# A Mamba-and-FFN block on one core: x*D joins the transposed y on the matrix engine, and the gate product moves from GpSimd to VectorE

## The chip, the cores and the metric

The kernel runs on one core of a Trainium2 chip. The core has five engines that run side by side and meet only through semaphores: PE (TensorE, matrix products into PSUM), DVE (VectorE), ACT (ScalarE), POOL (GpSimd, which cannot reach PSUM here) and SP, whose queue issues most of the transfers. The metric is the device time of one execution in microseconds (us); lower is better.

## The reference, cut to what matters

Four sequences of 1024 tokens with 512 features pass an FFN with ternary weights, a Mamba layer, and the same FFN again. The part around the change is the end of the Mamba layer, for 1024 inner channels (E) and 16 states (N):

```python
def step(h, inp):
    d_l, B_l, C_l, x_l = inp
    A_bar = jnp.exp(d_l[:, :, None] * A)
    h = h * A_bar + (d_l * x_l)[:, :, None] * B_l[:, None, :]
    y_l = jnp.einsum('ben,bn->be', h, C_l)
    return (h, y_l)
...
y_apply_D = y + x * W_D
y_skip = y_apply_D * _silu(skip)
return resid + y_skip @ W_out
```

## The kernel before, in words

The 4096 tokens are cut into 16 chunks of 256 (`CH`). A software pipeline treats three chunks in one round: `PREV` jobs finish chunk i-1, `THIS` jobs belong to chunk i, `NEXT` jobs prepare chunk i+1. The rounds are called fill, first, loop (14 times, i = 1 to 14), last and drain. Each round has 32 slots. The tables `LOOP_SLOTS`, `FIRST_SLOTS` and so on set, slot by slot, which jobs PE runs, and the other engines derive their own fixed order from the same tables. Nothing is reordered at run time.

A job on PE fills one of four PSUM banks (`NBANK`). `bank_ready[bk]` tells that PE has filled it, `bank_used[bk]` that its reader is done. Names of jobs: `U1_p`/`G1_p` and `U2_p`/`G2_p` are the FFN's up and gate products (line 1596), `DN1`/`DN2` the down products (line 1607), `IN_q` and `SK_q` the projections to x and to the skip gate (line 1619), `DB` the projection to delta, B and C (line 1629), `OM_t` the output projection (line 1668).

The scan runs in 32 steps per chunk (`STEPS`): 16 states for the first half of the channels, then 16 for the second. For each step POOL writes u*B into the ring `h` (line 778; line 784 adds the carried state), DVE scans it in two pieces (line 1342), and then there are two ways to C*h. In most steps PE transposes h (line 1553) and DVE adds it with its C to `y` (line 1364). In the steps listed in `ELEM` (nine per chunk, the last of the first half being step 15, the last of the second half step 31) POOL multiplies h by a plane of C (line 795) and a transfer that it issues adds the product to `xw` (line 799); `elem_added` tells of its landing. `xw` begins as x*D, written by ACT (line 980).

`y` has tokens on partitions, everything else channels. So each half of `y` is transposed back at its end by PE, in four quarters of 256 channels, jobs `YT_0` to `YT_3` (line 1659): four 128x128 transposes each. In the loop `YT_0` stands in slot 20, `YT_1` in slot 21, `YT_2` in slot 4 and `YT_3` in slot 5 of the next round. DVE adds the bank to `xw` (`y_plus_x`, line 1433), POOL multiplies `xw` by the gate into `gz` (`gated`, line 906), and `out_proj` waits for that with `z_ready`.

POOL also forms the low half `hl` of the hidden activations (line 884), once DVE has multiplied the gate product in (line 1380) and ACT has written the high half `hh` (line 1064). Its orders tie POOL to PE: POOL's `hl` of `G1_7` comes in slot 11, after PE's `G1_7` in slot 10, and the product and transfer of step 15 in POOL's slot 19. Likewise `hl` of `G1_1` comes in POOL's slot 2, and step 31 in slot 3.

Of the kernel before, what the change touches and what calls it, by code (L numbers as in the profile page):

```python
# [21 lines left out]
P = 128  # L22
D, E, F, N, DD = 512, 1024, 2048, 16, 128
# [3 lines left out]
CH = 256  # L27
TB = CH // P
NCH = TOK // CH
# [15 lines left out]
QT = EB // 2  # L45
# [265 lines left out]
def after(ph, name, lag, s):  # L311

    return name in PHASES[ph] and s == USE_OF[ph][name] + lag
# [37 lines left out]
def elems_before(c, s):  # L351

    whole = [len(elem_of(k)) for k in range(c)]
    return sum(whole) + sum(k < s for k in elem_of(c))
# [38 lines left out]
def job_no(ph, i, name):  # L393

    p = BANK_OF[ph][name]
    size = {f: len(JOBS[f, p]) for f in PHASES}
    before = JOBS[ph, p].index(name)
    if ph != "fill":
        before += size["fill"]
    if ph == "loop":  # L400
        before = before + size["first"] - size["loop"] + size["loop"] * i
    elif ph in ("last", "drain"):
        before += size["first"] + size["loop"] * (NCH - 2) + (size["last"] if ph == "drain" else 0)
    return p, before


def phase_of(c):

    return "first" if c == 0 else ("last" if c == NCH - 1 else "loop")
# [27 lines left out]
    return 2 * NCH - 1 + (0 if ph == "last" else 1)  # L437


def need(eng, sem, value):  # L440

    if isinstance(value, int) and value <= 0:
        return
    eng.wait_ge(sem, value)


def macaron_kernel(nc, resid, norm_w, W_skip, W_in, conv_w, conv_b, W_delta_1, W_delta_2, b_delta_2, W_B, W_C,
# [3 lines left out]
    ALU = mybir.AluOpType  # L451
# [8 lines left out]
    with ctx:  # L460
# [3 lines left out]
        def sem(name):  # L464
            return ctx.enter_context(nc.semaphore(name))
# [18 lines left out]
        ident = sb("ident", [P, P])  # L484
# [45 lines left out]
        xw = sb("xw", [P, EB, CH])  # L530
        gz = sb("gz", [P, EB, CH])
# [8 lines left out]
        y = sb("y", [P, TB, HE * P])  # L540
# [19 lines left out]
        bank_ready = [sem(f"bank_ready{p}") for p in range(NBANK)]  # L560
# [16 lines left out]
        conv_begun, conv_step, edge_added = sem("conv_begun"), sem("conv_step"), sem("edge_added")  # L577
        ctanh_ready, xc_ready, xw_ready = sem("ctanh_ready"), sem("xc_ready"), sem("xw_ready")
        sp_step, delta_ready, u_ready = sem("sp_step"), sem("delta_ready"), sem("u_ready")
        gtanh_ready, z_ready = sem("gtanh_ready"), sem("z_ready")  # L580
        pool_go, dve_go, act_go = sem("pool_go"), sem("dve_go"), sem("act_go")
        pe_go, sp_go = sem("pe_go"), sem("sp_go")

# [151 lines left out]
        def _(pool):  # L735
# [4 lines left out]
            pl = nc.gpsimd  # L740
# [151 lines left out]
                pl.tensor_tensor(u[:, :, :], delta[:, half * HE:(half + 1) * HE, :],  # L892
                                 xc[:, half * HE:(half + 1) * HE, :], ALU.mult).then_inc(u_ready, 1)

            def gated(ph, i, q):

                bk, before = job_no(ph, i, f"YT_{q}")
                need(pool, bank_used[bk], before + 1)
                gate = f"SK_{q}"
                if q < 2:  # L900
                    bk, before = job_no(ph, i, gate)
                else:
                    bk, before = job_no(phase_of(i - 1), i - 1, gate)
                need(pool, bank_used[bk], before + 1)
                qb = slice(2 * q, 2 * q + 2)
                pl.tensor_tensor(gz[:, qb, :], xw[:, qb, :], gz[:, qb, :], ALU.mult).then_inc(z_ready, 1)  # L906

            def run(ph, i):
                has = PHASES[ph]
                scan = "SK_0" in has  # L910
                next_ln = NEXT_LN_FILL if ph == "fill" else NEXT_LN
                for s in range(STEPS):
                    coming, done = step_of(ph, i, s + U_AHEAD), step_of(ph, i, s)
                    if coming and s not in UB_LATE:
                        u_times_b(*coming)
                    if done and is_elem(*done) and s not in ELEM_LATE:
                        state_times_c(*done)
                    if s == EDGES_AT and "IN_0" in has:
                        edges(i + 1)
                    for half in range(2):  # L920
                        if after(ph, f"IN_{2 * half + 1}", 0, s):
                            add_edges(ph, i, half)
                    if after(ph, "OM_1", 0, s):
                        rstd(ph, i, "2")
                    for q in range(QT):
                        if after(ph, f"YT_{q}", 0, s):
                            gated(ph, i, q)
                    for kind, p in hidden_units(ph, s):
                        hidden_low(ph, i, kind, p)
                    if after(ph, "DN1_1", 0, s):  # L930
                        rms(ph, i)
                    if ph != "fill" and after(ph, "D2_1", 2, s):
                        softplus(i + 1, 0)
                    if ph != "fill" and after(ph, "D2_1", 3, s):
                        first_state(i + 1, 0)
                    if after(ph, "D2_3", 2, s):
                        softplus(i, 1)
                    if after(ph, "D2_3", 3, s):
                        first_state(i, 1)
                    if s == next_ln and "T1_0" in has:  # L940
                        rstd(ph, i, "n")
                    if coming and s in UB_LATE:
                        u_times_b(*coming)
                    if done and is_elem(*done) and s in ELEM_LATE:
                        state_times_c(*done)
# [8 lines left out]
        def _(sc):  # L954
# [19 lines left out]

            def x_times_d(i, half):

                need(sc, z_ready, 4 * i - 2 + 2 * half)
                need(sc, xc_ready, 2 * i + 2)
                for b in range(half * HE, (half + 1) * HE):
                    ins = ac.activation(xw[:, b, :], xc[:, b, :], ACT.Copy, scale=wd[:, b:b + 1])  # L980
                ins.then_inc(xw_ready, 1)
# [266 lines left out]
        def _(ve):  # L1248
# [173 lines left out]
                gg = gz[:, 2 * q:2 * q + 2, :].rearrange("p e t -> p (e t)")  # L1422
                v.scalar_tensor_tensor(out=gg, in0=gg, scalar=1.0, in1=pp, op0=ALU.add, op1=ALU.mult).then_inc(bank_used[bk], 1)

            def y_plus_x(ph, i, q):

                bk, pp = ready(ph, i, f"YT_{q}")
                qb = slice(2 * q, 2 * q + 2)
                c = i if q < 2 else i - 1
                need(ve, xw_ready, 2 * c + q // 2 + 1)  # L1430
                need(ve, elem_added, 16 * elems_before(c, N * (q // 2 + 1)))
                yx = xw[:, qb, :]
                ins = v.tensor_tensor(yx.rearrange("p e t -> p (e t)"), pp, yx.rearrange("p e t -> p (e t)"), ALU.add)  # L1433
                ins.then_inc(bank_used[bk], 1)

            def run(ph, i):
                if ph == "first":
# [28 lines left out]
            def use(ph, i, name):  # L1466

                nslot = (i + 1) % XSLOTS
                pslot = (i - 1) % XSLOTS
                t = int(name[-1]) if "_" in name else 0  # L1470
                if name[0] == "U":
                    hidden_up(ph, i, int(name[1]), t)
                elif name[0] == "G":
                    hidden_gate(ph, i, int(name[1]), t)
                elif name[:2] in ("T1", "T2"):
                    x_low(ph, i, int(name[1]), t)
                elif name[:2] == "OM":
                    need(ve, x12_ready, i)
                    add_to_stream(ph, i, name, pslot, 0.5)
                    stats(ph, i, "2", pslot, t)  # L1480
                    if t:
                        moments(ph, i, "2")
                elif name[:3] == "DN1":
                    add_to_stream(ph, i, name, nslot, down_sc[:, 0:1])
                    stats(ph, i, "p", nslot, t)
                    if t:
                        moments(ph, i, "p")
                elif name[:3] == "DN2":
                    add_to_stream(ph, i, name, pslot, down_sc[:, 0:1])
                elif name[:2] == "SK":  # L1490
                    skip_gate(ph, i, t)
                elif name[:2] == "YT":
                    y_plus_x(ph, i, t)

            def background(ph, i, s):

# [19 lines left out]
        def _(pe):  # L1516
# [135 lines left out]
            def y_T(ph, i, q):  # L1652
                c = i if q < 2 else i - 1
                for t in range(TB):
                    need(pe, y_added[t], rows_before(c, N * (q // 2 + 1)))
                bk, pp = opened(ph, i, f"YT_{q}")
                for e in range(2):
                    for t in range(TB):
                        ins = te.transpose(pp[:, e * CH + t * P:e * CH + (t + 1) * P],
                                           y[:, t, (2 * (q % 2) + e) * P:(2 * (q % 2) + e + 1) * P], ident[:, :])  # L1660
                ins.then_inc(bank_ready[bk], 1)

            def out_proj(ph, i, name, lo, hi):
                t = int(name[3])
                bk, pp = opened(ph, i, name, lo)
                need(pe, z_ready, 4 * i - 3 + (hi - 1) // 2)
                for e in range(lo, hi):
                    ins = te.matmul(pp, gz[:, e, t * P:(t + 1) * P], w_out[:, e, :], start=(e == 0), stop=(e == EB - 1))  # L1668
                if hi == EB:
                    ins.then_inc(bank_ready[bk], 1)  # L1670
# [94 lines left out]
```

## Time and profile before

| what | value |
|---|---|
| median of 3 runs | 2801.0 us (2798.93 to 2805.9) |
| profiled execution, first to last instruction | 2796.2 us |
| PE busy | 2614.3 us (93%) |
| DVE busy | 2447.7 us (88%) |
| POOL busy | 2382.1 us (85%) |
| ACT busy | 1879.0 us (67%) |
| mean granted PE clock | 0.979 of 2.4 GHz |

The profiled execution is known by its span; the timed runs have no trace. Busy time is the union of an engine's instructions. A matmul on f32 operands appears as two records, one on 16-bit or 8-bit operands, or a transpose, as one. The duration of a PE record contains its latency, so that records overlap; what a matmul occupies is read from how far apart the starts of equal ones lie. In the chain of work that ended last, pieces of one kind are merged and do not overlap.

### The profile page before, as it was taken

To read this page: it belongs to the slowest core of one execution; us is meant where nothing else is said; L and a number is where in the kernel's file an instruction comes from. 1 tells how busy PE (TensorE), PEld (TensorE's weight loads), DVE (VectorE), ACT (ScalarE), POOL (GpSimd) and SP (SyncE) were. 2 spreads that over 40 slices of the span, in tenths; PEclk is the share of its full clock that TensorE was granted. 3 is DMA by queue.
4 is the path that set the end of the run, shared out by engine and by line. 5 is a ranking of instruction groups with operands and counts; after the bars stand their busy time and mean duration, and the time that the engine had idled before them with its cause. 6 is when DMAs were issued, how large, how long until landed. Compare 5 with 4: busy or idle time off the path is not lost.

```text
span 2796.2 us, 51718 instructions
## 1 busy us (share of the span) xinstructions
PE 2614.3 (93%) x17439; PEld 2021.6 (72%) x17439; DVE 2447.7 (88%) x3221; ACT 1879.0 (67%) x4340; POOL 2382.1 (85%) x2023
## 2 busy tenths in 40 slices
PE   5776899999999999999999999999999999999878
PEld 4555677777878777786777778677777877776655
DVE  4378899999999999899999999899999999999892
ACT  7374867676676767667676766767676676767651
POOL 1168899999898999999998999999999898999881
PEclk9898999999999999999999999999999999999989
DMA  7013222223222322222232222222222222222220
GB/s 274 31 55 72 60 61 76 56 58 83 59 74 60 80 50 65 77 63 73 58 81 53 70 69 63 73 63 75 54 72 66 66 69 65 73 57 68 64 55 8
DMA packets 94446, 192.44 MB, mean 69 GB/s; under 512 B 12588, under 2 KB 32232, under 8 KB 93672
## 3 DMA queue, kind: packets, MB, share of 16 engines
q0 software_dynamic: 20304, 73.93, 13.7%
q1 hardware_dynamic: 73880, 115.21, 13.0%
q8 instruction: 141, 2.31, 0.3%
q14 instruction: 121, 0.99, 0.1%
HBM read 106.26 MB, written 8.91 MB: 41 GB/s over the span
## 4 chain that ended last, share of the span: by engine, by line
POOL 41%; PE 32%; issue 12%; DVE 7%; ACT 2%; DMA 1%; POOLq 1%; DVEq 0%; ACTq 0%
POOL h L778 22%; PE ps L1596 10%; POOL h L795 7%; PE ps L1607 6%; PE ps L1619 6%; POOL hl L884 4%; PE ps L1553 4%; PE ps L1668 4%; DVE h L1342 3%; POOL u L892 2%; POOL delta L849 2%; DVE xc L1400 1%; PE ps L1629 1%; POOL h L784 1%; POOL xw L799 1%
## 5 line engine op out<-in xcount | busy, mean ns | idle before, releaser
L778 POOL TENSOR_TENSOR h<-u,bb 128x1024 f32<-128x1024 f32 x512 | 1257.8, 2466 | 27.2 <-DVE u L1417 14.2
L1342 DVE TENSOR_TENSOR_SCAN h<-ps,h 128x512 f32<-128x512 f32 x1024 | 1191.8, 1207 | 36.5 <-POOL h L784 18.6
L1037 ACT ACTIVATE ps<-delta,a_neg 128x255 f32<-128x255 f32 x2048 | 873.1, 468 | 377.0 <-DVE h L1342 374.8
L1596 PE MATMUL ps<-xh,q_up 128*128 128x256 f16 x2048 | 466.5, 275 | 36.1 <-DVE xl L1280 19.1
L1364 DVE SCALAR_TENSOR_TENSOR y<-ps,ccur,y 128x512 f32<-128x512 f32 x678 | 471.4, 738 | 6.9 <-PE ps L1553 6.3
L1596 PE MATMUL ps<-xh,q_gate 128*128 128x256 f16 x2048 | 462.7, 273 | 8.1 <-DVE xw L1433 7.8
L1596 PE MATMUL ps<-xl,q_up 128*128 128x256 f16 x2048 | 466.5, 275 | 0.0
L1596 PE MATMUL ps<-xl,q_gate 128*128 128x256 f16 x2048 | 462.4, 273 | 0.0
L1553 PE MATMUL ps<-ident,h 128*128 128x128 f32 x2968 | 398.2, 277 | 50.2 <-DVE y L1364 46.7
L1553 PEld LDWEIGHTS ps<-ident,h 128*128 128x128 f32 x2968 | 344.6, 142 | 112.7 <-issue 50.9
L884 POOL TENSOR_TENSOR hl<-act,hh 128x512 f16<-128x512 f32 x256 | 314.5, 1229 | 97.3 <-ACT hh L1064 94.4
L1607 PE MATMUL ps<-q_down,hh 128*128 128x512 fp8e4 x1024 | 388.6, 379 | 2.5 <-POOL hl L884 1.2
L1607 PE MATMUL ps<-q_down,hl 128*128 128x512 fp8e4 x1024 | 388.5, 379 | 0.0
L795 POOL TENSOR_TENSOR h<-h,cplane 128x1024 f32<-128x1024 f32 x141 | 334.8, 2374 | 0.0
L1059 ACT ACTIVATE act<-ps,tanh_sc 128x512 f32<-128x512 f32 x256 | 174.9, 683 | 201.1 <-PE ps L1596 129.0
L1372 DVE SCALAR_TENSOR_TENSOR act<-act,ps 128x512 f32<-128x512 f32 x256 | 173.6, 678 | 98.3 <-ACT act L1059 97.9
L1596 PEld LDWEIGHTS ps<-xh,q_up 128*128 128x128 fp8e4 x2048 | 201.6, 98 | 76.8 <-issue 51.8
L1619 PE MATMUL ps<-xrT,w_in 128*128 128x256 f32 x1024 | 235.3, 384 | 13.5 <-DVE xc L1400 11.2
L1668 PE MATMUL ps<-w_out,gz 128*128 128x512 f32 x512 | 243.5, 609 | 2.3 <-POOL gz L906 2.2
L1596 PEld LDWEIGHTS ps<-xh,q_gate 128*128 128x128 fp8e4 x2048 | 200.9, 98 | 39.8 <-issue 15.0
L1619 PE MATMUL ps<-xrT,w_skip 128*128 128x256 f32 x1024 | 229.5, 379 | 0.0
L1596 PEld LDWEIGHTS ps<-xl,q_up 128*128 128x128 fp8e4 x2048 | 201.6, 98 | 33.5 <-issue 4.6
(126 smaller groups left out, 3642.9 us busy)
## 6 DMA issues: line engine op xcount, KB each, us to landing
xw<-h POOLq DMA_DIRECT2D x141, 512.0 KB, 4.5
bb<-b_scratch SPq DMA_DIRECT2D x224, 256.0 KB, 3.1
cplane<-c_scratch SPq DMA_DIRECT2D x141, 128.0 KB, 3.1
xs<-in_L_attn_resid_dram SPq DMA_DIRECT2D x17, 512.0 KB, 3.5
out_dram<-xs SPq DMA_DIRECT2D x15, 512.0 KB, 4.3
wraw<-in_L_ffn_W_up_dram SPq DMA_DIRECT2D x4, 1024.0 KB, 9.6
wraw<-in_L_ffn_W_gate_dram SPq DMA_DIRECT2D x4, 1024.0 KB, 12.3
wraw<-in_L_ffn_W_down_dram SPq DMA_DIRECT2D x4, 1024.0 KB, 14.1
```

What stands on the lines that cost most here:

```text
L778: ins = pl.tensor_tensor(hs, u[:, :, :], bb[:, q % 2, s % PLANES:s % PLANES + 1, :].broadcast_to([P, HE, CH]), ALU.mult)
L795: pl.tensor_tensor(hs, hs, cplane[:, k:k + 1, :].broadcast_to([P, HE, CH]), ALU.mult).then_inc(times_c, 1)
L884: pl.tensor_tensor(hl[:, 2 * p:2 * p + 2, :], act[:, p % ACTS, :].rearrange("q (f t) -> q f t", f=2), hh[:, 2 * p:2 * p + 2, :], ALU.subtr ...
L1037: ins = ac.activation(abar[r][:, e, 1:], delta[:, k, 1:], ACT.Exp, scale=a_neg[:, k, n:n + 1])
L1059: ac.activation(act[:, p % ACTS, :], pp, ACT.Tanh, scale=tanh_sc[:, 0:1]).then_inc(tanh_ready, 1)
L1342: v.tensor_tensor_scan(hr, abar[r].rearrange("p e t -> p (e t)"), hr, 0.0, ALU.mult, ALU.add).then_inc(scanned, 1)
L1364: ins = v.scalar_tensor_tensor(out=yy, in0=hT[:, t, :], scalar=cc, in1=yy, op0=ALU.mult, op1=ALU.add)
L1553: ins = te.transpose(hT[:, t, e * P:(e + 1) * P], h[:, (STEPS * i + s) % RING, e, t * P:(t + 1) * P], ident[:, :])
L1596: ins = te.matmul(pp[:, f * CH:(f + 1) * CH], w[:, d, col:col + P], part[:, d, :], start=(d == 0 and part is xh), stop=(d == DB - 1 and pa ...
L1607: ins = te.matmul(pp, part[:, f, t * P:(t + 1) * P], q_down[:, f, :], start=(f == 0 and part is hh), stop=(f == FB - 1 and part is hl))
L1619: ins = te.matmul(pp[:, e * CH:(e + 1) * CH], w[:, d, col:col + P], xrT[:, d, :], start=(d == 0), stop=(d == DB - 1))
L1668: ins = te.matmul(pp, gz[:, e, t * P:(t + 1) * P], w_out[:, e, :], start=(e == 0), stop=(e == EB - 1))
```

## The change

The x*D with the elementwise states (`xw`) is no longer added by DVE. PE makes each quarter's transposition as four ordinary f32 products with the identity, the first of which opens the bank's accumulation, waits for `xw_ready` and `elem_added`, and adds `xw` by a fifth product, identity times `xw`, 128x512 in f32. DVE then multiplies the bank by the gate straight into `gz`, and POOL's product is gone with its semaphore. `out_proj` now waits for DVE's `bank_used`, and ACT's `x_times_d` for PE's `bank_ready` of the quarters of the chunk before.

```diff
-            def gated(ph, i, q):
...
-                pl.tensor_tensor(gz[:, qb, :], xw[:, qb, :], gz[:, qb, :], ALU.mult).then_inc(z_ready, 1)
...
             def x_times_d(i, half):
-                need(sc, z_ready, 4 * i - 2 + 2 * half)
+                if i:
+                    for q in (2 * half, 2 * half + 1):
+                        bk, done = y_T_of(i - 1, q)
+                        need(sc, bank_ready[bk], done + 1)
...
-            def y_plus_x(ph, i, q):
+            def gated(ph, i, q):
                 bk, pp = ready(ph, i, f"YT_{q}")
...
-                need(ve, xw_ready, 2 * c + q // 2 + 1)
-                need(ve, elem_added, 16 * elems_before(c, N * (q // 2 + 1)))
-                yx = xw[:, qb, :]
-                ins = v.tensor_tensor(yx.rearrange("p e t -> p (e t)"), pp, yx.rearrange("p e t -> p (e t)"), ALU.add)
-                ins.then_inc(bank_used[bk], 1)
+                gate, done = job_no(ph, i, f"SK_{q}") if q < 2 else job_no(phase_of(i - 1), i - 1, f"SK_{q}")
+                need(ve, bank_used[gate], done + 1)
+                gg = gz[:, 2 * q:2 * q + 2, :].rearrange("p e t -> p (e t)")
+                v.tensor_tensor(gg, pp, gg, ALU.mult).then_inc(bank_used[bk], 1)
...
             def y_T(ph, i, q):
...
-                        ins = te.transpose(pp[:, e * CH + t * P:e * CH + (t + 1) * P],
-                                           y[:, t, (2 * (q % 2) + e) * P:(2 * (q % 2) + e + 1) * P], ident[:, :])
+                        te.matmul(pp[:, e * CH + t * P:e * CH + (t + 1) * P],
+                                  y[:, t, (2 * (q % 2) + e) * P:(2 * (q % 2) + e + 1) * P], ident[:, :], start=(e, t) == (0, 0), stop=False)
+                need(pe, xw_ready, 2 * c + q // 2 + 1)
+                need(pe, elem_added, 16 * elems_before(c, N * (q // 2 + 1)))
+                ins = te.matmul(pp, ident[:, :], xw[:, 2 * q:2 * q + 2, :].rearrange("p e t -> p (e t)"), start=False, stop=True)
                 ins.then_inc(bank_ready[bk], 1)
...
             def out_proj(ph, i, name, lo, hi):
...
-                need(pe, z_ready, 4 * i - 3 + (hi - 1) // 2)
+                gate, done = y_T_of(i - 1, (hi - 1) // 2)
+                need(pe, bank_used[gate], done + 1)
```

The slot tables are the same, so every job keeps its place. On PE, in a loop round, around `YT_2` and `YT_3` (ahead of them stands the gate product `G1_3`, between them the transposes of one scan step, behind them `U1_4`), there stood before:

```order
L1596 MATMUL ps<-xl,q_gate 128x256
L1659 MATMUL ps<-ident,y 128x128 x4
L1553 MATMUL ps<-ident,h 128x128 x8
L1659 MATMUL ps<-ident,y 128x128 x4
L1596 MATMUL ps<-xh,q_up 128x256
```

and there stand now (line 1650 is the four products on y, line 1654 the one on xw):

```order
L1587 MATMUL ps<-xl,q_gate 128x256
L1650 MATMUL ps<-ident,y 128x128 x4
L1654 MATMUL ps<-xw,ident 128x512
L1544 MATMUL ps<-ident,h 128x128 x8
L1650 MATMUL ps<-ident,y 128x128 x4
L1654 MATMUL ps<-xw,ident 128x512
L1587 MATMUL ps<-xh,q_up 128x256
```

Two 128x512 products have come in, each behind a wait for the transfers into xw, and everything behind them on PE waits with them.

On POOL, in a loop round, at the place of `YT_0` and `YT_1` (from the last transfer of the first half on), there stood before:

```order
L799 DMA xw<-h 128x1024
L884 TENSOR_TENSOR hl<-act,hh 128x512
L778 TENSOR_TENSOR h<-u,bb 128x1024
L784 TENSOR_TENSOR h<-h,a 128x4
L877 TENSOR_TENSOR xc<-xc,edge 128x4x3
L906 TENSOR_TENSOR gz<-xw,gz 128x512
L778 TENSOR_TENSOR h<-u,bb 128x1024
L784 TENSOR_TENSOR h<-h,a 128x4
L795 TENSOR_TENSOR h<-h,cplane 128x1024
L799 DMA xw<-h 128x1024
L906 TENSOR_TENSOR gz<-xw,gz 128x512
```

The two rows of line 906 are gone and the rest stands in the same order.

## Rows read from the trace of the kernel before

**Rows 1.** The page's head and its busy times.

```profile
span 2796.2 us, 51718 instructions
PE 2614.3 (93%) x17439; PEld 2021.6 (72%) x17439; DVE 2447.7 (88%) x3221; ACT 1879.0 (67%) x4340; POOL 2382.1 (85%) x2023
```

**Rows 2.** The page's chain that ended last, by engine.

```profile
POOL 41%; PE 32%; issue 12%; DVE 7%; ACT 2%; DMA 1%; POOLq 1%; DVEq 0%; ACTq 0%
```

**Rows 3.** Busy time, ten rounds: length, PE, PEld, DVE, ACT, POOL, granted clock, DMA share.

```profile
400.00:2025.60 1625.60, 1598.51 (x10763) 1240.43 (x10762) 1503.75 (x1981) 1142.15 (x2684) 1499.20 (x1274) 1.00 0.27 67
```

**Rows 4.** Timeline of PE (start, length): YT_0 of rounds 1 and 11.

```profile
399.88 0.60 PE L1659 MATMUL ps<-ident,y 128*128 128x128 f32 x4
...
2025.49 0.60 PE L1659 MATMUL ps<-ident,y 128*128 128x128 f32 x4
```

**Rows 5.** Groups by line: busy us, mean ns, idle before it.

```profile
L906 POOL TENSOR_TENSOR gz<-xw,gz 128x512 f32<-128x512 f32 x64 | 81.9, 1314 | 25.5 <-DVE xw L1433 25.5
L1433 DVE TENSOR_TENSOR xw<-ps,xw 128x512 f32<-128x512 f32 x64 | 43.5, 682 | 5.5 <-DMA xw<-h 4.7 <-PE ps L1659 0.8
L1659 PE MATMUL ps<-ident,y 128*128 128x128 f32 x256 | 40.0, 281 | 8.9 <-DVE y L1364 4.7 <-ACT tmp L1116 3.7
```

**Rows 6.** Chain in order of time: start, us, records.

```profile
1007.28 0.86 PE ps L1668 x2
1008.14 0.88 PE ps L1553 x8
...
1022.43 6.91 PE ps L1619 x32
...
1079.70 4.35 PE ps L1629 x32
```

**Rows 7.** Timeline of POOL, round 5: hl of G1_7, and step 15's transfer.

```profile
1008.50 1.16 POOL L884 TENSOR_TENSOR hl<-act,hh 128x512 f16<-128x512 f32 x1
...
1049.22 0.89 POOL L799 DMA_DIRECT2D xw<-h  x1 [0.57 <-POOL h L795]
```

**Rows 8.** Timelines of DVE and ACT between G1_7 and that hl.

```profile
1003.50 0.69 DVE L1380 SCALAR_TENSOR_TENSOR act<-ps,act 128x512 f32<-128x512 f32 x1
1004.11 2.33 DVE L1342 TENSOR_TENSOR_SCAN h<-ps,h 128x512 f32<-128x512 f32 x2
...
1007.38 0.61 ACT L1064 ACTIVATE hh<-act 128x512 f16<-128x512 f32 x1
```

**Rows 9.** Timeline of PE, round 5: first product behind G1_7, and YT_0.

```profile
1003.22 0.38 PE L1607 MATMUL ps<-q_down,hh 128*128 128x512 fp8e4 x1
...
1050.01 0.60 PE L1659 MATMUL ps<-ident,y 128*128 128x128 f32 x4
```

**Rows 10.** The page's transfers: issues, KB each, median us to landing.

```profile
xw<-h POOLq DMA_DIRECT2D x141, 512.0 KB, 4.5
```

**Rows 11.** Timelines of POOL and PE: step 31's transfer, and YT_2.

```profile
969.38 0.89 POOL L799 DMA_DIRECT2D xw<-h  x1 [0.57 <-ACT carry L1043]
...
971.76 0.63 PE L1659 MATMUL ps<-ident,y 128*128 128x128 f32 x4
```

**Rows 12.** The same two for step 15 and YT_0 of round 4.

```profile
885.62 0.88 POOL L799 DMA_DIRECT2D xw<-h  x1 [0.57 <-POOL h L795]
...
888.19 0.60 PE L1659 MATMUL ps<-ident,y 128*128 128x128 f32 x4
```

**Rows 13.** Two idle times of PE, and busy times with granted clock around each.

```profile
737.73 2.64 PE L1619 MATMUL ps<-xrT,w_in 128*128 128x256 f32 x11 [1.98 <-DVE xc L1400]
2581.50 1.22 PE L1553 MATMUL ps<-ident,h 128*128 128x128 f32 x8 [4.14 <-DVE y L1364]
...
733.00:753.00 20.00, 17.76 (x136) 14.38 (x134) 19.82 (x30) 12.95 (x31) 17.54 (x14) 1.00 0.31 66
2577.00:2600.00 23.00, 13.03 (x54) 7.64 (x52) 17.34 (x19) 14.09 (x40) 21.05 (x16) 0.85 0.40 103
```

**Rows 14.** Who ended PE's idle time before line 1668.

```profile
  POOL gz L906: 9.6, 16
```

More of the change, by code:

```diff
@@ L437, in rstd_run, with y_T_of @@
     return 2 * NCH - 1 + (0 if ph == "last" else 1)
+def y_T_of(c, q):
+    i = c if q < 2 else c + 1
+    ph = {0: "first", NCH - 1: "last", NCH: "drain"}.get(i, "loop")
+    return job_no(ph, i, f"YT_{q}")
 def need(eng, sem, value):
@@ L579, in macaron_kernel @@
         sp_step, delta_ready, u_ready = sem("sp_step"), sem("delta_ready"), sem("u_ready")
-        gtanh_ready, z_ready = sem("gtanh_ready"), sem("z_ready")
+        gtanh_ready = sem("gtanh_ready")
         pool_go, dve_go, act_go = sem("pool_go"), sem("dve_go"), sem("act_go")
@@ L893, in u_of @@
                                  xc[:, half * HE:(half + 1) * HE, :], ALU.mult).then_inc(u_ready, 1)
-            def gated(ph, i, q):
[L897 to L905, printed above, removed]
-                pl.tensor_tensor(gz[:, qb, :], xw[:, qb, :], gz[:, qb, :], ALU.mult).then_inc(z_ready, 1)
             def run(ph, i):
@@ L924, in run @@
                         rstd(ph, i, "2")
-                    for q in range(QT):
-                        if after(ph, f"YT_{q}", 0, s):
-                            gated(ph, i, q)
                     for kind, p in hidden_units(ph, s):
@@ L1423, in skip_gate @@
                 v.scalar_tensor_tensor(out=gg, in0=gg, scalar=1.0, in1=pp, op0=ALU.add, op1=ALU.mult).then_inc(bank_used[bk], 1)
-            def y_plus_x(ph, i, q):
+            def gated(ph, i, q):
                 bk, pp = ready(ph, i, f"YT_{q}")
-                qb = slice(2 * q, 2 * q + 2)
-                c = i if q < 2 else i - 1
-                need(ve, xw_ready, 2 * c + q // 2 + 1)
-                need(ve, elem_added, 16 * elems_before(c, N * (q // 2 + 1)))
-                yx = xw[:, qb, :]
-                ins = v.tensor_tensor(yx.rearrange("p e t -> p (e t)"), pp, yx.rearrange("p e t -> p (e t)"), ALU.add)
-                ins.then_inc(bank_used[bk], 1)
+                gate, done = job_no(ph, i, f"SK_{q}") if q < 2 else job_no(phase_of(i - 1), i - 1, f"SK_{q}")
+                need(ve, bank_used[gate], done + 1)
+                gg = gz[:, 2 * q:2 * q + 2, :].rearrange("p e t -> p (e t)")
+                v.tensor_tensor(gg, pp, gg, ALU.mult).then_inc(bank_used[bk], 1)
             def run(ph, i):
@@ L1492, in use @@
                 elif name[:2] == "YT":
-                    y_plus_x(ph, i, t)
+                    gated(ph, i, t)
             def background(ph, i, s):
```

## The prediction

> **What bounds the kernel now.** I began with the page's busy times [rows 1]: PE, DVE and POOL all stand between 85% and 93%, so the average decides nothing. The chain that ended last runs 41% through POOL and only 32% through PE [rows 2], which would make POOL the engine to relieve. But such a chain follows one of several paths of nearly equal length, so I looked at the steady rounds alone. Two equal events ten rounds apart give the round: (2025.49 - 399.88)/10 = 162.56 us [rows 4]. In the same ten rounds PE is busy for 1598.5 of 1625.6 us at full clock: 2.7 us of idle time in a round [rows 3]. DVE has 12.2 us and POOL 12.6 us. PE's records overlap, so its busy time might flatter it; but starts lie as close as the column count allows (next part), so PE is really streaming. PE is the fullest engine and has 2.7 us to give; POOL is tied to it through the ring and through `hl`, which is how the chain comes to run there.
>
> **The change part by part.**
>
> *POOL loses 64 products.* They are 81.9 us busy and had 25.5 us of waiting before them [rows 5], in a steady round 4 x 1.3 = 5.1 us. That is 5.1 us more of slack on an engine that already has 12.6.
>
> *DVE swaps one operation for another.* The add of a bank and an SBUF tile, 128x512 f32, takes 682 ns [rows 5]; the product has the same operands and sizes. Price 0. Its wait for the transfers (4.7 us in all) goes, and comes back on PE.
>
> *PE gets the work.* Prices come from pieces of the chain [rows 6]. An f32 product of 512 columns is two records in 0.86 us; 256 columns: 16 products in 6.91 us, 0.432 each; 160 columns: 16 products in 4.35 us, 0.272 each. That is 1.69 ns a column at all three sizes. Transposes of 128 columns go at 0.88/8 = 0.11 us. An f32 product of 128 columns does not occur in the steady rounds. Below it cannot beat the column law, 0.218 us; above, the product of 160 columns, with the same size of weights, bounds it at 0.272. I take 0.218, since all three sizes lie on the law. A quarter then costs 4 x 0.218 + 0.86 - 4 x 0.11 = 1.29 us more (1.51 at the upper bound). A round has four: 5.2 us (6.0). I add 0.2 us a round for the extra switches between operand types, an allowance of mine, bounded by the same 0.8.
>
> A page's rule speaks here. The Trainium skill, page "TensorE: Matmul & The Clock Gate", section "Terms", says that transpose mode is four times faster for FP32, while the rows say twice (0.218 against 0.11). By the page's factor a product would take 0.44 us and a quarter 2.18 us; no f32 product of 128 columns is in this trace, but the one of 160 columns at 0.272 contradicts it.
>
> *PE waits for the transfers.* The fifth product now stands in PE's queue behind `elem_added`, and the next gate product, then everything else, stands behind it. YT_0 in round 5: step 15's transfer is issued at 1049.22 [rows 7], lands a median 4.5 us later [rows 10], at 1053.7. PE starts YT_0 at 1050.01 [rows 9] and with the slower products is ready for the fifth at 1050.88. So PE would wait 2.8 us. Can POOL, with its new slack, be earlier? POOL's 40.7 us from `hl` of G1_7 to that issue [rows 7] are a closed run of its own work and contain none of the removed products. That `hl` starts at 1008.50, and its input ends at 1007.99 [rows 8]: it can move by 0.5 us. The input itself hangs on PE: DVE's product starts with the end of G1_7 (behind it PE's next job starts at 1003.22 [rows 9]), then come DVE's scan of the next step (2.33 us), ACT's exponentials and `hh`, in fixed order [rows 8]. So this wait is not a matter of load but of a path from PE back to PE: 1003.2 to 1053.7 is 50.5 us, less 0.5, against 47.7 us of PE's own work. The wait is 2.3 us. In the three rounds that begin a sequence (4, 8, 12) POOL has no line 784 and issues earlier: 885.62 + 4.5 = 890.1 against 888.19 + 0.87 = 889.1 [rows 12], 1.0 us. Mean over 14 rounds: (11 x 2.3 + 3 x 1.0)/14 = 2.0 us; I take 2.2, since some landings will be later than the median. YT_1 needs no later transfer and does not wait.
>
> YT_2: issued at 969.38, landed at 973.9; PE starts at 971.76 and is ready at 972.63 [rows 11]. 1.3 us, and again a short path from G1_1 through DVE, ACT and POOL's `hl`, in which POOL may gain about half a microsecond. I take 0.7 us (0 to 1.3).
>
> *What is given back.* PE no longer waits for POOL's product ahead of `out_proj`: 9.6 us in 16 rounds, 0.6 a round [rows 14]. Some of the other 2.1 us of PE's idle time will shrink as DVE and POOL have more slack; but idle time inside the two paths above gives nothing, since the wait grows by as much. I take 0.8 in all (0 to 2).
>
> *ACT's wait* moves from `z_ready` to `bank_ready` of jobs that ended at least three slots before. Price 0.
>
> *Sum.* A loop round: 5.2 + 0.2 + 2.2 + 0.7 - 0.8 = 7.5 us, 14 rounds 105 us. Eight of the 64 quarters lie in first, last and drain, 8 x 1.29 = 10.3 us, where PE is not full; I take 8. Together +113 us against the span of 2796.2, giving 2909. The median of the runs shown lies 4.8 us above that span, so the time is 2801 + 113 = 2914 us.
>
> **The rivals.**
>
> *POOL leads and the waits vanish.* If the lighter POOL ran 2 to 3 us further ahead, only the work would stay: 5.2 - 0.8 + 0.2 = 4.6 a round, 64 us, plus 8: 2873 us; with the waits half gone, 2893. For it: POOL would be relieved by 5.1 us just where the chain runs. Against: the closed run of POOL work above, and its start tied to G1_7.
>
> *The clock falls.* PE idle for 1.98 us kept full clock; after idling 4.14 us the stretch around it shows 0.85 of it [rows 13], between the levels 2.4 and 1.2 GHz: 0.15 x 23 = 3.4 us lost. The new wait of 2.3 us lies nearer to the first row. If every YT_0 did as the second, 14 x 3.4 = 48 us more: 2962. A late landing in a round or two could do it there alone, for 3 to 7 us.
>
> *The dearer product.* With 0.272 us it is 14 us more: 2928. By a factor of four, taken as a mechanism of this kernel, 4 x (0.44 - 0.218) x 64 = 57 us more: 2971. The product of 160 columns speaks against it. This is the page's rule above.
>
> *Not slower.* POOL is the pacer, as the chain suggests, PE's added work hides in its idle time, and the round becomes shorter by POOL's 5.1 us: 14 x 5.1 = 71 us, 2730. It would need PE to take 5.2 us more inside a round of 157.5 us, where it now fills 159.9. With PE's extra work just covered, the time stays 2801. It decides if PE has more than 5.2 us free per round; the rows give 2.7.
>
> **How the numbers follow.** The forecast with its waits (2890 to 2945): 0.60. Waits mostly gone (2865 to 2890): 0.20. Clock or dearer product (2945 to 2975): 0.14. Not slower, 0.04; something I have missed above that, 0.02. The range 2868 to 2955 goes from the vanishing waits, nearly bare, to the forecast with the dearer product and both waits unhelped: 14 x (6.0 + 2.6 + 1.3) + 10 = 149, with 4.8 us of clock loss. About 0.3% (8 us) is what a measurement of this kernel can tell from no change. Faster by more than that 0.02, within it 0.03, slower 0.95.
>
> **What would show each step right or wrong.** After the change the ten rounds should give about 170 us a round. PE's idle time before the fifth product should be near 2.2 us at YT_0 and 0.7 us at YT_2, released by the transfer into `xw`, shorter in rounds 4, 8 and 12. The fifth product should occupy 0.86 us, the four before it 0.22 each. POOL's idle time should rise by about 12 us a round, and the chain should pass through the transfer once a round. No idle time before the fifth product would speak for the first rival; a granted clock under 1.00 in rounds 2 to 14 for the second; a distance of 0.27 or 0.44 us between the products on y for the third; a round of 163 us or less would make the whole reading wrong.

## The result, and the profile after

The changed kernel takes 2943.0 us (median of 4 runs, 2942.5 to 2944.5) against 2800.8 before: a ratio of 1.051, 95% interval 1.049 to 1.052, so 142 us slower. The forecast was 113 us slower, 2914 us, with a range of 2868 to 2955 that holds the result.

The page of the changed kernel, its head, its busy times and the chain that ended last by engine:

```profile
span 2941.5 us, 52422 instructions
PE 2721.4 (93%) x17823; PEld 2090.7 (71%) x17823; DVE 2457.5 (84%) x3221; ACT 1882.0 (64%) x4340; POOL 2314.9 (79%) x1959
...
POOL 47%; PE 22%; issue 14%; DVE 6%; DMA 3%; ACT 2%; POOLq 1%; DVEq 0%; ACTq 0%
```

Beside [rows 1]: PE is busy for 107 us more, POOL for 67 us less, DVE for 10 and ACT for 3 us more. Beside [rows 2] the chain leans on POOL even more, though POOL has less to do, and the share of transfers in it has gone from 1% to 3%. A chain through POOL did not mean that work taken from POOL would shorten it.

The timeline of PE at YT_0 of rounds 1 and 11, and the busy times between them (columns as in [rows 3]):

```profile
410.63 0.61 PE L1650 MATMUL ps<-ident,y 128*128 128x128 f32 x4
...
2131.02 1.05 PE L1650 MATMUL ps<-ident,y 128*128 128x128 f32 x8
...
410.60:2131.00 1720.40, 1661.92 (x11001) 1280.55 (x11001) 1511.45 (x1981) 1144.42 (x2684) 1458.29 (x1234) 0.99 0.26 63
```

A round is (2131.02 - 410.63)/10 = 172.0 us, 9.5 us longer than by [rows 4]; 14 such rounds are 133 of the 142 us. PE's idle time is 5.8 us a round instead of 2.7, POOL's 26.2 instead of 12.6. The clock (the seventh figure) is 0.99 where it was 1.00.

The groups by line that answer to [rows 5] (busy us, mean ns, idle before it):

```profile
L1654 PE MATMUL ps<-xw,ident 128*128 128x512 f32 x128 | 73.3, 656 | 56.6 <-DMA xw<-h 56.6
L1650 PE MATMUL ps<-ident,y 128*128 128x128 f32 x512 | 72.1, 286 | 5.3 <-DVE y L1358 4.7
L1403 DVE SCALAR_TENSOR_TENSOR xc<-tmp,xc 128x1024 f32<-128x1024 f32 x32 | 47.1, 1473 | 10.9 <-ACT tmp L1091 10.9
L1355 DVE TENSOR_SCALAR y<-ps,ccur 128x512 f32<-128x512 f32 x64 | 45.1, 746 | 88.6 <-PE ps L1654 88.6
L1425 DVE TENSOR_TENSOR gz<-ps,gz 128x512 f32<-128x512 f32 x64 | 43.4, 680 | 20.1 <-PE ps L1654 19.9
```

DVE's product costs 680 ns where the add cost 682. PE waits 56.6 us for the transfers into `xw`. One round in order of time, POOL's `hl` of G1_7 and its transfer of step 15, then PE's four products and the fifth (start, length, idle time before it):

```profile
1403.70 1.16 POOL L891 TENSOR_TENSOR hl<-act,hh 128x512 f16<-128x512 f32 x1
...
1444.40 0.89 POOL L806 DMA_DIRECT2D xw<-h  x1 [0.57 <-POOL h L802]
...
1445.36 1.05 PE L1650 MATMUL ps<-ident,y 128*128 128x128 f32 x8
1449.00 1.10 PE L1654 MATMUL ps<-xw,ident 128*128 128x512 f32 x2 [2.58 <-DMA xw<-h]
```

POOL's run from `hl` to the issue is 40.7 us, the same as in [rows 7]; 4.6 us later the transfer has landed and PE goes on.

### The profile page after: what moved, and what is told of

Same layout as the page of the kernel before. It is cut to its first block, busy times and chain, and to the rows that moved or that the text cites. A ratio compares the mean times of both kernels' runs of the same rounds, so it can differ in the third digit from the quotient of the medians.

```text
span 2941.5 us, 52422 instructions
## 1 busy us (share of the span) xinstructions
PE 2721.4 (93%) x17823; PEld 2090.7 (71%) x17823; DVE 2457.5 (84%) x3221; ACT 1882.0 (64%) x4340; POOL 2314.9 (79%) x1959
## 3 DMA queue, kind: packets, MB, share of 16 engines
q8 instruction: 144, 2.36, 0.3%
## 4 chain that ended last, share of the span: by engine, by line
POOL 47%; PE 22%; issue 14%; DVE 6%; DMA 3%; ACT 2%; POOLq 1%; DVEq 0%; ACTq 0%
POOL h L785 28%; POOL h L802 7%; PE ps L1587 7%; POOL hl L891 4%; PE ps L1598 4%; DMA xw<-h 3%; PE ps L1610 3%; PE ps L1663 3%; PE ps L1544 3%; DVE h L1336 2%; POOL u L899 2%; POOL delta L856 2%; DVE xc L1394 2%; PE ps L1654 1%; POOL h L791 1%
## 5 line engine op out<-in xcount | busy, mean ns | idle before, releaser
L891 POOL TENSOR_TENSOR hl<-act,hh 128x512 f16<-128x512 f32 x256 | 308.5, 1205 | 252.5 <-ACT hh L1058 250.1
L1587 PE MATMUL ps<-xh,q_gate 128*128 128x256 f16 x2048 | 471.3, 276 | 0.3 <-DVE wscale L1281 0.3
L1587 PE MATMUL ps<-xl,q_gate 128*128 128x256 f16 x2048 | 471.0, 276 | 0.0
L1587 PEld LDWEIGHTS ps<-xl,q_gate 128*128 128x128 fp8e4 x2048 | 203.1, 99 | 40.6 <-issue 10.3
```

What stands on the lines that cost most here:

```text
L891: pl.tensor_tensor(hl[:, 2 * p:2 * p + 2, :], act[:, p % ACTS, :].rearrange("q (f t) -> q f t", f=2), hh[:, 2 * p:2 * p + 2, :], ALU.subtr ...
L1587: ins = te.matmul(pp[:, f * CH:(f + 1) * CH], w[:, d, col:col + P], part[:, d, :], start=(d == 0 and part is xh), stop=(d == DB - 1 and pa ...
```

## The experiments

The ratio of each is to runs of the kernel before on the same chip (2801.7 to 2802.5 us). "Work" is what PE got to do, "wait" is the transfer it waits for. Some versions leave a part of the result out, to price one thing alone; the texts in front of them say so.

**The fifth product without its wait.** In the changed kernel:

```diff
-                need(pe, xw_ready, 2 * c + q // 2 + 1)
-                need(pe, elem_added, 16 * elems_before(c, N * (q // 2 + 1)))
-                ins = te.matmul(pp, ident[:, :], xw[:, 2 * q:2 * q + 2, :].rearrange("p e t -> p (e t)"), start=False, stop=True)
+                ins = te.matmul(pp, ident[:, :], w_skip[:, 0, 0:512], start=False, stop=True)
```

> The changed kernel, but the fifth product multiplies the identity by a constant tile (the first 512 columns of w_skip) and waits neither for xw_ready nor for elem_added. What it leaves out: x*D and the elementwise states do not reach the output. PE's work is the same to the instruction. Theory W (work plus a wait for the transfer, on a path from PE's G1_7 and G1_1 back to PE): the 56.6 us of idle time before the fifth product vanish and with them the six falls of the clock in the rounds of the loop (3.4 us each at half speed, 1.7 us lost each); 2943 - 57 - 10 = 2876 us, so 2801 + 75. Rival P (PE's added work is nearly all of it, and the waits only take the place of other idle time): 2920 or more. Rival D (DVE's wait for the bank before it starts the next half of y, 88.6 us in the changed kernel, is what costs): this wait shrinks only a little here, 2920 or more as well.

2867.3 us, ratio 1.023 (1.022 to 1.025). The work is worth 65 us, the wait the other 76. The busy times of its page, and a piece of its chain in order of time, which prices the products:

```profile
PE 2695.1 (94%) x17823; PEld 2074.8 (72%) x17823; DVE 2457.7 (86%) x3221; ACT 1882.1 (66%) x4340; POOL 2318.1 (81%) x1959
...
1073.07 0.89 PE ps L1650 x8
1073.96 0.86 PE ps L1652 x2
```

Four f32 products of 128 columns take 0.89 us, 0.222 each, and the one of 512 columns 0.86 us: a quarter costs 0.89 + 0.86 - 0.44 = 1.31 us more, 64 of them 84 us. 65 us arrived. PE's idle time fell from 2796.2 - 2614.3 = 182 us to 2865.4 - 2695.1 = 170, so part of the rest went there. Rival P is out, and so is D as it was put: DVE's wait for the bank did not stay, it fell from 88.6 to 48.6 us together with PE's own. The clock fell eight times in the rounds of the changed kernel, not six as the expectation has it, and not once here.

**The wait without the work.** In the kernel before:

```diff
                 for e in range(2):
                     for t in range(TB):
+                        if (e, t) == (1, TB - 1):
+                            need(pe, xw_ready, 2 * c + q // 2 + 1)
+                            need(pe, elem_added, 16 * elems_before(c, N * (q // 2 + 1)))
                         ins = te.transpose(...)
```

> The kernel before with one thing more: PE waits for xw_ready and elem_added ahead of the last transpose of each quarter, as the changed kernel does ahead of its fifth product. No work is added, POOL and DVE do what they did. Theory W: PE's path through G1_7, POOL and the transfer back to YT_0 is 3.1 us longer than PE's own and that through G1_1 to YT_2 1.5 us, less what POOL can gain (0.3 to 0.5): 14 x (2.8 + 1.2) = 56 us and some clock falls, 2802 + 60 = 2862 us. Rival P (the wait only takes the place of other idle time): 2802 to 2825 us.

2880.1 us, ratio 1.028 (1.027 to 1.030): 78 us, more than the 60 expected; rival P is out. The two halves meet, 65 + 78 = 143 for the 142 of the whole, but that they meet so closely is in part luck: the wait is not quite the same in both. Here PE comes to it sooner, waits 74.7 us instead of 56.6, and the clock of the span is 0.968 instead of 0.974. The line of its transposes in the view by source (who ended PE's idle time, us, times):

```profile
  DMA xw<-h: 74.7, 30
```

**The four products alone.** The kernel before with `te.matmul` in place of `te.transpose` in `y_T`, nothing else.

> The kernel before with only the four transposes of each quarter made ordinary f32 products with the identity; no fifth product, no further wait. Nothing is left out. By the sum of the prediction: 64 x 4 x (0.218 - 0.11) = 28 us if all of it lies on the path, 2802 + 25 = 2827 us. Rival (PE's idle time takes it up): 2802 to 2810. Rival (weights of an f32 product set the pace, 0.272 us each): 2840.

2813.9 us, ratio 1.005 (1.003 to 1.006): 12 us. Their own price is 64 x (0.89 - 0.44) = 29 us, so less than half of it reached the end. Expected were 25, and 0 to 8 by the rival with PE's idle time; the truth lies between, nearer to the rival. By difference the fifth product then has 65 - 12 = 53 of its 64 x 0.86 = 55 us on the path: the first microseconds of added work were largely taken up, the later ones hardly.

**Half of the change: POOL keeps the gate.** In the kernel before, `y_T` as in the changed kernel, and

```diff
-                need(ve, xw_ready, 2 * c + q // 2 + 1)
-                need(ve, elem_added, 16 * elems_before(c, N * (q // 2 + 1)))
-                ins = v.tensor_tensor(yx.rearrange("p e t -> p (e t)"), pp, yx.rearrange("p e t -> p (e t)"), ALU.add)
+                ins = v.tensor_copy(yx.rearrange("p e t -> p (e t)"), pp)
```

> One half of the change alone: PE adds xw by the identity as in the changed kernel, DVE only copies the bank to xw, and POOL multiplies by the gate as before. Nothing is left out. Theory W: POOL has 12 us a round idle in the changed kernel and the product lies outside the paths from G1_7 and G1_1; out_proj gets its 0.6 us wait a round back; 2943 to 2955 us, I say 2950. Rival Q (relief of POOL already pays for part of PE's work in the changed kernel): 14 x 2 to 14 x 5 more, 2970 to 3010 us.

2940.4 us, ratio 1.049 (1.048 to 1.051), 2.6 us below the changed kernel and below the 2943 to 2955 expected; rival Q is out. Taking 82 us of work from POOL bought nothing that can be told from noise. The next two runs show that two effects hide in this zero.

**POOL relieved and nothing else.** The kernel before without the gate: DVE's add writes into `gz`, POOL does nothing in its place.

```diff
-                ins = v.tensor_tensor(yx.rearrange("p e t -> p (e t)"), pp, yx.rearrange("p e t -> p (e t)"), ALU.add)
+                v.tensor_tensor(gg, pp, yx, ALU.add).then_inc(bank_used[bk], 1)
...
-                pl.tensor_tensor(gz[:, qb, :], xw[:, qb, :], gz[:, qb, :], ALU.mult).then_inc(z_ready, 1)
```

> The kernel before with POOL's gate product taken out and nothing put in its place: transposes as before, DVE adds the bank and xw and writes the sum into gz, out_proj waits for DVE. What it leaves out: the multiplication by the gate. It measures what relieving POOL by 5.1 us a round is worth by itself. Theory W: POOL has slack, only the wait ahead of out_proj goes (9.6 us in all) and little else; 2785 to 2801 us, I say 2792. Rival Q (POOL paces the rounds, as the chain's 41% suggests): up to 14 x 5.1 = 71 us less, 2730 to 2760 us.

2845.6 us, ratio 1.016 (1.014 to 1.017): 43 us slower with less work on POOL. Both theories were wrong. Timelines of this kernel, DVE and then POOL, right behind YT_1 (the first POOL row stands a little earlier, for the usual length of line 791):

```profile
1075.86 4.24 DVE L1403 SCALAR_TENSOR_TENSOR xc<-tmp,xc 128x1024 f32<-128x1024 f32 x1
...
1071.50 0.21 POOL L791 TENSOR_TENSOR h<-h,a 128x4 f32<-128x4 f32 x1
...
1075.25 1.46 POOL L891 TENSOR_TENSOR hl<-act,hh 128x512 f16<-128x512 f32 x1
1076.37 2.64 POOL L785 TENSOR_TENSOR h<-u,bb 128x1024 f32<-128x1024 f32 x1
1079.09 1.08 POOL L791 TENSOR_TENSOR h<-h,a 128x4 f32<-128x4 f32 x1
```

DVE's silu of x, two inputs in SBUF, starts beside POOL's `hl`, does not get in between that and POOL's product into `h`, and ends 1.1 us behind the product's end (1079.01). POOL's small operation of line 791, 0.21 us elsewhere, takes 1.08 us there and ends with the silu: the holding up goes both ways. In the kernel before the same place reads:

```profile
1060.88 1.22 DVE L1409 SCALAR_TENSOR_TENSOR xc<-tmp,xc 128x1024 f32<-128x1024 f32 x1
...
1061.38 0.89 POOL L799 DMA_DIRECT2D xw<-h  x1 [0.57 <-DVE xc L1400]
1062.79 1.26 POOL L906 TENSOR_TENSOR gz<-xw,gz 128x512 f32<-128x512 f32 x1 [0.53 <-DVE xw L1433]
```

There POOL only issued a transfer and then waited for DVE's add before its gate product. The Trainium skill, page "SBUF — State Buffer", section "Terms", calls the pair of ports that DVE and GpSimd share "Lock-allocated, exclusive, held for the full instruction": these rows fit it.

**The same, and POOL waits.** `e2_relief` with one wait on POOL and no work behind it:

```diff
+                    for q in range(QT):
+                        if after(ph, f"YT_{q}", 0, s):
+                            bk, before = job_no(ph, i, f"YT_{q}")
+                            need(pool, bank_used[bk], before + 1)
```

> The kernel without POOL's product and without the gate (e2_relief), but POOL waits at the old place of the product until DVE is done with that bank, and computes nothing there. What it leaves out: the gate multiplication, as in e2_relief. In e2_relief DVE's line 1403 (x's silu, two inputs in SBUF, 1.2 us in the kernel before) takes 4.0 to 6.4 us in every round, for as long as POOL's products last, one behind the other; in the kernel before POOL stood idle there, waiting for DVE. Theory S (DVE is held up while POOL works with two SBUF inputs, and POOL's wait is what kept it free): line 1403 returns to 1.2 us, the time to 2785 to 2802 us. Rival R (e2_relief is slow because DVE writes gz and x_times_d and out_proj wait for DVE in another way): it stays at 2845 us or gets worse by the waits, up to 2860.

2796.7 us, ratio 0.998 (0.997 to 0.999); rival R is out. A wait without work, at four places of POOL's round, is worth 49 us. The silu's group in `e2_relief` and, behind it, here:

```profile
L1403 DVE SCALAR_TENSOR_TENSOR xc<-tmp,xc 128x1024 f32<-128x1024 f32 x32 | 89.7, 2803 | 10.9 <-ACT tmp L1091 10.9
```

```profile
L1407 DVE SCALAR_TENSOR_TENSOR xc<-tmp,xc 128x1024 f32<-128x1024 f32 x32 | 42.1, 1317 | 10.9 <-ACT tmp L1095 10.9
```

The groups differ by 47.6 us, nearly all of the 49: it is the first of the two silus in a round that takes 3.9 to 6.4 us there and 1.2 here. With the collision out of the way, relieving POOL is worth 5 us (2 to 7 by the interval).

**DVE does both operations.** Whole versions without any work for PE. First, behind the add, and with POOL's wait as above:

```diff
+                need(ve, bank_used[bk], job_no(ph, i, f"YT_{q}")[1] + 1)
+                gate, done = job_no(ph, i, f"SK_{q}") if q < 2 else job_no(phase_of(i - 1), i - 1, f"SK_{q}")
+                need(ve, bank_used[gate], done + 1)
+                v.tensor_tensor(gz[:, qb, :], yx, gz[:, qb, :], ALU.mult).then_inc(z_ready, 1)
```

> A whole version that leaves nothing out: transposes and the add on DVE as before, then DVE also multiplies by the gate (xw and gz, both in SBUF), and POOL only waits for DVE's add at the old place. POOL is relieved by 5.1 us a round, DVE gets 4 x 0.7 us and may be held up by POOL at each of the four (up to 2.4 us each). Theory W: PE has 2.7 us a round of idle time, so the gain is bounded by 38 us and will be small; 2790 to 2810 us if DVE's product is not held up. If it is held up in most rounds: 2810 to 2850. Rival Q (POOL paces the rounds): 2740 to 2770.

2843.3 us, ratio 1.015 (1.013 to 1.016), within what was expected for a product that is held up; rival Q is out. The product takes 0.69 us at the median and up to 3.29. Second, with the sum left in PSUM, so that neither operation has two inputs in SBUF:

```diff
-                ins = v.tensor_tensor(yx.rearrange("p e t -> p (e t)"), pp, yx.rearrange("p e t -> p (e t)"), ALU.add)
+                v.tensor_tensor(pp, pp, yx.rearrange("p e t -> p (e t)"), ALU.add).then_inc(sum_ready, 1)
...
+                v.tensor_tensor(gg, pp, gg, ALU.mult).then_inc(bank_used[bk], 1)
```

> A whole version that leaves nothing out. Transposes as before; DVE adds xw to the bank in place (PSUM and SBUF in, PSUM out) and then multiplies the bank by the gate into gz (PSUM and SBUF in), so that neither operation reads two tiles from SBUF; POOL only waits at the old place until DVE is done with the bank. Theory S (what holds DVE up is a DVE instruction with two inputs in SBUF while POOL works): DVE's product costs its 0.7 us and no more, x's silu stays at 1.2 to 1.3 us, and the time lies between that of e5_relief_wait (2797) and 12 us above it; I say 2803. Rival (DVE's extra 2.7 us a round are what made e6_dve_both_wait slow, held up or not): 2835 to 2845 us.

2828.9 us, ratio 1.010 (1.008 to 1.012): 14 us better than through SBUF, but 27 above the kernel before; 2803 were expected, 2835 to 2845 by the rival, and the truth lies between. The product is held up no more (0.69 us on average), but its 44 us cost 32 against `e5_relief_wait`, though DVE has 12 us idle in a round. DVE's idle time did not take the work up; at which wait it is paid was not measured.

Third, the second without POOL's wait:

> As e9_dve_psum, but POOL does not wait for DVE at the place of its old product. Nothing is left out. Theory S: POOL's products come one behind the other again while DVE wants to run x's silu (two inputs in SBUF), which takes 4 us and more in every round as in e2_relief: 2840 to 2860 us. Rival (the silu's length has another cause than POOL's work, and a wait more or less on POOL changes nothing): as e9_dve_psum, within 5 us.

2865.9 us, ratio 1.023 (1.021 to 1.025), 37 us above its twin and 6 above the range expected; the silu is back at 2504 ns on average (1316 with the wait), 38 us in all. A second pair says the same of the wait.

**Other work while the transfer lands.** The changed kernel with YT_0 alone moved in the loop's table:

```diff
-    ["YT_0", "G2_1", ("IN_0", 0, 2)],
+    ["G2_1", ("IN_0", 0, 1), "YT_0", ("IN_0", 1, 2)],
```

> The changed kernel with YT_0 alone moved behind G2_1 and half of IN_0 (3.5 us later on PE), YT_2 and YT_3 in their old places. Nothing is left out. In e4_later the wait for the transfer was nearly gone too, but PE then waited 2.4 us a round for DVE's up product ahead of a gate product (0 in the changed kernel), which I put down to DVE waiting for YT_3 behind U1_4. Theory W: here 2.6 us a round at YT_0 and most clock falls go, YT_2 keeps its 1.3 us, no new wait: 2943 - 14 x 2.6 - 8 = 2899 us. Rival P (the time saved at YT_0 reappears at DVE or at the product's bank): 2920 to 2940 us.

2898.9 us, ratio 1.035 (1.033 to 1.036), as expected to the microsecond. PE's wait for the transfers is down from 56.6 to 22.0 us, and the clock stays at 1.00 through the loop. With YT_2 and YT_3 moved as well:

```diff
-    ["D2_3", "G1_3", "YT_2"],
-    ["YT_3", "U1_4", "G1_4"],
+    ["D2_3", "G1_3"],
+    ["U1_4", "YT_2", "YT_3", "G1_4"],
```

> The changed kernel with YT_0 moved behind G2_1 and half of IN_0 in slot 20 of the loop (3.5 us later on PE), and YT_2 and YT_3 moved into slot 5 behind U1_4 (YT_2 later by a step's transposes and U1_4, 2.6 us). Nothing is left out. Theory W: PE does other work while the transfer lands, the idle time before the fifth product goes from 56.6 us to under 10 us, clock falls go; 2943 - 47 - 10 = 2886 us if DVE, whose next half of y waits for these banks, does not become late; up to 2910 if it does. Rival P: 2930 to 2945, the idle time shows up elsewhere on PE.

2930.1 us, ratio 1.046 (1.044 to 1.047): 31 us worse than with YT_0 alone, far from the 2886 expected and where rival P had it. The wait for the transfers is at 9.0 us, but PE has a new one; the view of its waits (total us, times, longest):

```profile
PE ps L1587 <- DVE act L1366: 37.8, 28, 2.4
```

It is 4.9 us in the changed kernel. Timelines of DVE and PE in one round, then the busy times behind the same wait in this round and the next:

```profile
1016.68 1.41 DVE L1355 TENSOR_SCALAR y<-ps,ccur 128x512 f32<-128x512 f32 x2 [2.35 <-PE ps L1654]
1018.01 0.68 DVE L1366 SCALAR_TENSOR_TENSOR act<-act,ps 128x512 f32<-128x512 f32 x1
...
1018.83 0.27 PE L1587 MATMUL ps<-xh,q_gate 128*128 128x256 f16 x1 [2.36 <-DVE act L1366]
...
1018.00:1028.00 10.00, 9.17 (x63) 7.46 (x64) 8.29 (x12) 6.09 (x10) 4.84 (x5) 0.83 0.08 28
1191.00:1201.00 10.00, 9.73 (x72) 7.61 (x73) 9.85 (x14) 5.30 (x10) 6.08 (x5) 1.00 0.08 28
```

DVE may not begin the next half of `y` until PE has read the old one. It stands in its fixed order 2.35 us for `YT_3`, and the up product behind it (line 1366), for which PE waits, comes late by as much. This idle time of PE is 2.36 us in every one of the 14 rounds; behind ten of them the clock falls for a while, 1.7 us lost each, and behind four it does not. So of the 31 us about half are the clock's.

## Why the prediction was right, step by step

*PE is the fullest engine, and the POOL chain misleads.* Shown: taking away POOL's work lost 3 us in one pair (`e3_pool_gates` and the changed kernel) and gained 5 in another (the kernel before and `e5_relief_wait`). The sum gave POOL's relief no more than a part of the 0.8 us under "given back", for a good reason and with one thing overlooked: POOL's slack is useless, and a part of the old product's use was its wait, which kept POOL from holding DVE up. The prediction saw only the first. The changed kernel escapes most of the second: the first silu of a round takes 1.58 us where it took 1.22, and its group averages 1473 ns where the kernel before has 1356:

```profile
L1409 DVE SCALAR_TENSOR_TENSOR xc<-tmp,xc 128x1024 f32<-128x1024 f32 x32 | 43.4, 1356 | 12.2 <-ACT tmp L1097 12.2
```

In `e3_pool_gates`, where POOL still waits, it is 1306 ns, 5.3 us in all less than in the changed kernel; that is about what the relief gives.

*The price of the products.* Right: 0.222 and 0.86 us against 0.218 and 0.86. The factor of four that the Trainium skill states for transpose mode (page "TensorE: Matmul & The Clock Gate", section "Terms") is two here, 0.222 against 0.11 us. The step from price to time was a little high, 65 us measured for the work, where the terms for work, less what is given back, came to 14 x 4.6 + 8 = 72.

*The wait for the transfer.* Right in place, way and reason, too small in size. This is the term that was mis-sized: 14 x (2.2 + 0.7) = 41 us forecast, 76 measured. PE's idle times before the fifth product show a part of it. At YT_0 they add up to 33.6 us in the 14 rounds, 2.4 a round; a regular round waits 2.6 us where the text had 2.3, and rounds 4, 8 and 12 wait 1.0 to 1.3 us, where 1.0 was forecast. In some rounds POOL's run to the issue is longer (41.2 us before the wait of 3.04 us in round 5, below, 41.5 before one of 3.36 us in round 13); late landings are two, both in round 6, 6.0 and 5.0 us behind the issue where 4.6 is usual, and PE waits 2.7 and 3.0 us for them. POOL gained 0.2 of the half microsecond that I gave it: in round 7 its `hl` starts 5.1 us behind PE's first product after G1_7 (1398.59 to 1403.70), before the change it was 5.3 (1003.22 to 1008.50, [rows 7] and [rows 9]). At YT_2 the idle times add up to 17.0 us, 1.2 a round, as much as without any gain of POOL; timeline of PE, rounds 3 and 8:

```profile
672.02 1.13 PE L1650 MATMUL ps<-ident,y 128*128 128x128 f32 x8
674.12 1.10 PE L1654 MATMUL ps<-xw,ident 128*128 128x512 f32 x2 [0.96 <-DMA xw<-h]
...
1534.80 1.13 PE L1650 MATMUL ps<-ident,y 128*128 128x128 f32 x8
1537.14 1.10 PE L1654 MATMUL ps<-xw,ident 128*128 128x512 f32 x2 [1.21 <-DMA xw<-h]
```

Outside the loop there are two more, 6.0 us, which the sum had at nothing. That makes the 56.6 us. The rest is the clock above all.

*The clock.* I gave this rival a small chance as the full case, and it came in part. Timeline of PE at YT_0 in rounds 5 and 9, and the busy times behind it in rounds 5, 9 and 7 (the seventh figure is the granted clock):

```profile
1099.02 1.43 PE L1654 MATMUL ps<-xw,ident 128*128 128x512 f32 x2 [3.04 <-DMA xw<-h]
...
1788.93 1.84 PE L1654 MATMUL ps<-xw,ident 128*128 128x512 f32 x2 [2.58 <-DMA xw<-h]
...
1098.00:1108.00 10.00, 8.98 (x45) 6.85 (x46) 4.37 (x6) 0.97 (x3) 6.96 (x7) 0.83 0.35 85
1788.00:1798.00 10.00, 9.07 (x46) 6.75 (x47) 4.74 (x7) 1.32 (x6) 6.92 (x7) 0.83 0.32 79
1448.00:1458.00 10.00, 9.00 (x55) 7.23 (x56) 4.81 (x8) 2.99 (x11) 6.77 (x6) 1.00 0.37 88
```

Behind an idle time of 3.04 us the clock is 0.83 for 10 us, that is 1.7 us lost, partly at 1.2 GHz. But it is 0.83 behind the 2.58 us of round 9 too, and behind the 2.58 us of round 7 it stays at 2.4 GHz: the length of the idle time alone does not tell. Of the twelve idle times of 2.58 us and more in the loop eight are followed by such a fall. My argument that a wait of 2.3 us lies nearer to the 1.98 us that kept the clock did not hold. Over the whole span the clock is 0.974 against 0.980 in `e1_static`: (0.026 x 2941.5 - 0.020 x 2865.4) = 19 us more lost, 14 of them in the eight falls.

PE's idle time is 220 us against the 170 of `e1_static`, 50 more, so 7 of the 56.6 us took the place of other idle time. 50 + 19 = 69 of the 76 us that the wait is worth. For 5 of the other 7 I have an estimate: in the round shown above (1445.36) the record of the four products is 1.05 us long, but by `e1_static` a product could follow after 0.89, so each of the 30 waits would be 0.16 us longer than it looks. How much of the clock's loss lies on the path was not measured by itself.

*What POOL and DVE give back.* 0.8 us a round was forecast. The wait ahead of `out_proj` did go. Of the 84 us of work 84 - 65 = 19 did not arrive, 1.4 us a round; 12 of them are idle time that PE had before.

*DVE as a price of 0.* Its operation is, 680 ns against 682, but DVE now waits 88.6 us for PE before it starts the next half of `y`, where it had 0.4 us of idle time. It falls to 48.6 us without the transfer wait. That this is paid from slack in the changed kernel is my reading of DVE's idle time; no run isolates it. `e4_later` shows the same wait as a cost.

So the way and the mechanism are shown, by two kernels that each carry one half. That the time came inside the range is in part luck: the range's upper end was built from waits without POOL's help, which came, and from a dearer product, 11 us, which did not; what took its place were the falls of the clock and the waits outside the loop, for which the sum had nothing.

No version here beats the kernel before; `e5_relief_wait` is 0.2% faster, but it leaves the gate out. The changed kernel's best form is `e10_yt0_later`, still 3.5% behind.

## What to carry to other kernels

A chain that runs through an engine doesn't say that relief of this engine shortens it: look at which run of work is closed between two meetings with the fullest engine, and whether the removed instruction lies in it. Moving an operation onto an in-order engine moves its wait as well, and the wait may cost more than the work (76 against 65 us here). Before an instruction is taken out of a tuned program, ask what its wait did for others: here POOL's idle time ahead of its product was worth 49 us, in shorter DVE work.

## What the runs showed of the hardware that I had not expected

A DVE instruction with two inputs in SBUF took 1.2 us beside an idle POOL and 3.9 to 6.4 us (`e2_relief`) or 3.2 to 5.7 us (`e11_dve_psum_free`) where POOL ran product after product: it waited through several of them. DVE instructions of 512 columns with one input in PSUM kept their 0.66 to 0.75 us beside the same POOL work. Two pairs of kernels that differ in one kind of POOL wait differ by 49 and 37 us. An f32 product of 128 columns with fresh weights takes 0.222 us, what its columns ask for at the 1.69 ns a column of the longer ones. PE's idle times of 2.4 to 3.4 us in front of full streams bring the clock down for some microseconds in some rounds and not in others: behind 2.36 us in ten of 14 rounds of `e4_later`, behind 2.58 us in round 9 and not in round 7 of the changed kernel.
